# Routing and plan of the shared-and-routed layer inside the stage of its gated products

## What is computed

```
h_shared = swiglu(flat @ shared_in_w.T)          # swiglu(a, b) = silu(a) * b, hidden width 512
out_shared = h_shared @ shared_out_w.T + shared_out_b
g_idx = argmax(flat @ group_gate_w.T + group_bias)          # 2 groups
e_sel = (flat @ expert_gate_w.T)[group g_idx] + expert_bias[g_idx]   # 4 experts of the group
topv, topi = top_k(softmax(e_sel), 2); topv = topv / (sum(topv) + 1e-8)
h_expert = swiglu(flat @ expert_in_w.T)
out = out_shared + sum over the two chosen e: (topv_e * (h_expert @ expert_out_weight[e].T) + expert_out_bias[e])
```

## Time and profile before

| what | value |
|---|---|
| three runs | 3017.52, 3017.73, 3019.3 us |
| median | 3017.73 us |
| the profiled execution's own time | 3008.34 us |
| its span, first to last instruction | 3006.4 us |
| busy in the span: TensorE, VectorE, ScalarE, GpSimd | 80%, 51%, 39%, 17% |
| mean granted TensorE clock | 0.898 |

### The profile page before, as it was taken

The page is one execution under the profiler, slowest core; times in us unless marked ns, Lnnn a source line. Parts: engine busy times, 40 slices in busy tenths (PEclk is TensorE's granted clock), DMA queues, the critical chain, the costliest instruction groups (busy, mean ns, idle before and its releaser), DMA issues. The chain is left out here.

```text
span 3006.4 us, 52688 instructions
## 1 busy us (share of the span) xinstructions
PE 2412.4 (80%) x18555; PEld 2014.1 (67%) x18555; DVE 1548.0 (51%) x3102; ACT 1158.1 (39%) x2239; POOL 501.8 (17%) x812
## 2 busy tenths in 40 slices
PE   6989599769987859874976999999999999963266
PEld 4868499769965734764875777777777777753244
DVE  4646522232236651144445777777777777742455
ACT  3333222112213321122214666666666666624433
POOL 0000022112202100510001122222222222110043
PEclk9999699779988969976997999999999999976577
DMA  5000023134341121321665231335254452022144
GB/s 137 1 1 1 27 85 96 52 97 150 94 101 59 47 92 49 113 67 40 249 257 154 75 109 37 97 93 139 67 143 131 118 147 69 22 60 40 57 138 129
DMA packets 136391, 273.54 MB, mean 91 GB/s; under 512 B 33666, under 2 KB 70568, under 8 KB 133060
## 3 DMA queue, kind: packets, MB, share of 16 engines
q1 hardware_dynamic: 117332, 217.49, 23.2%
q0 software_dynamic: 18800, 52.69, 6.5%
HBM read 466.52 MB, written 65.74 MB: 177 GB/s over the span
## 5 line engine op out<-in xcount | busy, mean ns | idle before, releaser
L2245 PE MATMUL tx_ring<-g_ident,tx_p 128*128 128x128 f32 x2552 | 399.9, 284 | 40.9 <-DVE tx_p_t L2490 8.9
L2245 PEld LDWEIGHTS tx_ring<-g_ident,tx_p 128*128 128x128 f32 x2552 | 287.7, 142 | 147.3 <-DVE tx_p_t L2490 36.6
L2490 DVE COPY tx_p_t<-tx_ring 128x512 f32<-128x512 f32 x464 | 306.6, 686 | 147.3 <-PE tx_ring L2245 144.0
L2483 DVE TENSOR_REDUCE tx_neg_max<-tx_scores 128x1 f32<-128x1354 f32 x232 | 361.2, 1557 | 16.9 <-PE tx_scores L2233 16.7
L2379 ACT ACTIVATE tx_p<-tx_scores,tx_neg_max 128x1354 f32<-128x1354 f32 x232 | 322.6, 1390 | 104.2 <-DVE tx_neg_max L2483 103.9
L2233 PE MATMUL tx_scores<-tx_keys,tx_queries 96*128 96x512 f32 (+1 forms) x696 | 203.2, 401 | 14.5 <-DMA tx_queries<-tx_q_hi 11.2
L2386 ACT ACTIVATE tx_p_t<-tx_ring 128x384 f32<-128x384 f32 x232 | 113.4, 489 | 238.5 <-PE tx_ring L2245 235.3
L2285 PE MATMUL tx_ring<-tx_p_t,tx_values 128*32 128x128 f32 x5104 | 151.9, 274 | 17.4 <-ACT tx_p_t L2386 16.4
L2285 PEld LDWEIGHTS tx_ring<-tx_p_t,tx_values 128*32 128x32 f32 x5104 | 135.9, 110 | 28.3 <-ACT tx_p_t L2386 27.7
L2622 POOL TENSOR_SCALAR tx_std<-tx_mean_var 128x1 f32<-128x1 f32 x58 | 14.8, 256 | 769.5 <-DVE tx_mean_var L2554 403.0
L192 PE MATMUL ln_turned<-g_ident,g_xn 128*128 128x128 f32 x176 | 40.7, 419 | 117.8 <-DVE g_xn L179 117.8
(11 more groups left out here) (961 smaller groups left out, 5197.4 us busy)
## 6 DMA issues: line engine op xcount, KB each, us to landing
tx_keys<-expert_keys SPq DMA_DIRECT2D x696, 169.5 KB
lv1e_w<-in_L_ffn_W SPq DMA_DIRECT2D x232, 256.0 KB
tx_w<-in_L_ffn_W SPq DMA_DIRECT2D x58, 1024.0 KB
lv0e_w<-in_L_ffn_W SPq DMA_DIRECT2D x200, 256.0 KB
tx_values<-expert_values SPq DMA_DIRECT2D x58, 704.0 KB
tx_rows<-in_L_ffn_rows SPq DMA_DIRECT2D x29, 640.0 KB, 3.9
g_adj_t<-in_adj_t POOLq DMA_DIRECT2D x3, 3872.0 KB, 22.1
expert_values<-kv_v SPq DMA_DIRECT2D x8, 1408.0 KB
```

The lines of the kernel that those rows point to most:

```text
L2245: last = nc.tensor.transpose(ring[u % 2][:, (t - t0) * P:(t - t0 + 1) * P], p[n % 2][:, t * P:(t + 1) * P], g.ident[:])
L2483: nc.vector.tensor_reduce(neg_max[:, n % 4:n % 4 + 1], sc[n % 2][:, 0:N], AX_X, ALU.max, negate=True)\
L2490: nc.vector.tensor_copy(p_t[:, n % TURNED, t0:t0 + nt, :], ring[u % 2][:, 0:nt * P].rearrange("p (t q) -> p t q", q=P))\
```

## The change

The stages `srr` and `srp` are gone from `shared_and_routed`. Their instructions stand in a new class `Sorting`, whose methods are called inside `stage_gated_hidden`. TensorE runs the routing products first, then the products of slice 0, the counts, slice 1, four of the turned blocks, slice 2, the inversion of the sort and four more, slice 3 and the last three. VectorE's steps have become a generator that yields behind each step, and `take` draws steps up to a marker: up to "rank" ahead of the gated product of slice 0, up to "found" ahead of that of slice 1, and the rest ahead of that of slice 3. ScalarE's exponential, marks and copies stand between its silu instructions. The comparison `at_spot` is made in two halves. Counts, ranks, found places and logits share one bank of PSUM (`small`), and the turned coefficients use one bank (`turned`) in place of three. The helpers `top_two`, `softmax_to` and `divide_by_sum` became generators, which the other routing stages run to their end at once (`run`), so their instructions stay as they were.

```diff
@@ -1068,6 +1089,7 @@
     full = N // P
     with ExitStack() as ctx:
         s = Pool(nc, ctx, tag)
+        sort = Sorting(nc, g, s, *sorting)
         w, w_loaded = held.w_in, held.w_in_loaded
@@ -1086,14 +1108,17 @@
                 sync.dma_start(g.hidden_dram[b * P:b * P + n, :], h_rows[0:n, b % 3, :]).then_inc(kept[b % 3], 16)
             for k in range(3):
                 sync.wait_ge(kept[k], 16 * ((NB + 2 - k) // 3))
+            sort.rows_kept(sync, None)
 
         @block.gpsimd
         def _(pool):
+            sort.constants(pool)
             nc.gpsimd.memset(h[:, :, NT:NP], 0.0).then_inc(pad, 1)
             pool.wait_ge(pad, 1)
 
         @block.tensor
         def _(pe):
+            sort.pe_logits(pe)
             pe.wait_ge(w_loaded[0], 16)
             for j in range(HT):
@@ -1105,6 +1130,12 @@
                                                     w[0][:, k, half * HID + j * P:half * HID + (j + 1) * P],
                                                     src_t[:, k, c * CW:(c + 1) * CW], start=(k == 0), stop=(k == KD - 1))
                     last.then_inc(done, 1)
+                if j == 0:
+                    sort.pe_rank(pe)
+                if j == 2:
+                    sort.pe_found(pe)
+                if j:
+                    sort.pe_turn(pe, j - 1)
             pe.wait_ge(w_loaded[1], 16)
             for b in range(NB):
@@ -1122,12 +1153,18 @@
 
         @block.scalar
         def _(act):
+            sort.act_exp(act)
             for j in range(HT):
+                if j == 2:
+                    sort.act_marks(act)
+                if j >= 2:
+                    sort.act_turn(act, j - 2)
                 act.wait_ge(a_full, j + 1)
                 if j >= 2:
                     act.wait_ge(h_done, j - 1)
                 nc.scalar.activation(gate[j % 2][:].rearrange("p (c n) -> p c n", c=CH), wide[0][:, :, 0:CW], ACT.Silu)\
                     .then_inc(gate_done, 1)
+            sort.act_turn(act, 2)
             for b in range(NB):
                 act.wait_ge(rows_full, b + 1)
                 if b < 2:
@@ -1138,7 +1175,13 @@
 
         @block.vector
         def _(dve):
+            steps = sort.dve_steps(dve)
+            take(steps, 0, "rank")
             for j in range(HT):
+                if j == 1:
+                    take(steps, 0, "found")
+                if j == 3:
+                    take(steps, 1000)
                 dve.wait_ge(b_full, j + 1)
                 dve.wait_ge(gate_done, j + 1)
                 nc.vector.tensor_tensor(h[:, j, 0:NT].rearrange("p (c n) -> p c n", c=CH), wide[1][:, :, 0:CW],
@@ -1317,10 +1360,9 @@
                     pool.wait_ge(ones, 1)
 
             stage_norm(nc, g, "srn", g.xn, g.xn, g.xn_t, held.affine[:, 0:KD], held.affine[:, KD:2 * KD])
-            stage_route(nc, g, "srr", g.xn_t, experts + 2, "grouped", weights, counts,
-                        held=(held.gates, held.gates_loaded, held.gate_bias, 2))
-            stage_plan(nc, g, "srp", weights, counts[:, :, 0:experts], plan, coef=counts)
-        stage_gated_hidden(nc, g, "srh", g.xn_t, held, h)
+            sorting = (plan, g.xn_t, experts + 2, "grouped", weights, counts[:, :, 0:experts], counts,
+                       (held.gates, held.gates_loaded, held.gate_bias, 2))
+            stage_gated_hidden(nc, g, "srh", g.xn_t, held, h, sorting)
         stage_routed_tiles(nc, g, "sro", h, held, plan, a["L1_ffn_out_bias"])
 
 
@@ -1541,6 +1583,365 @@
+class Sorting:
...
+        self.small, self.turned = s.ps("small", [P, BANK]), s.ps("turned", [plan.width, BANK])
...
+    def pe_rank(self, pe):
+        nc, experts = self.nc, self.plan.experts
+        wide = (NB + 1) * experts
+        pe.wait_ge(self.shaped, 2)
+        pe.wait_ge(self.v_step, 1)
+        flat, counts = self.small[:, 0:wide], self.every[:].rearrange("p b e -> p (b e)")
+        nc.tensor.matmul(flat, self.upto[:], counts[:, NB * experts:], start=True, stop=False)
+        for shift in range(1, NB + 1):
+            before = (NB - shift) * experts
+            last = nc.tensor.matmul(flat, self.all_ones[:], counts[:, before:before + wide], start=False, stop=(shift == NB))
+        last.then_inc(self.rank_full, 1)
+    def pe_turn(self, pe, c):
+        nc = self.nc
+        b0, n = TG[c]
+        pe.wait_ge(self.v_step, 1)
+        if c:
+            pe.wait_ge(self.turned_read, c)
+        for b in range(b0, b0 + n):
+            last = nc.tensor.transpose(self.turned[:, (b - b0) * P:(b - b0 + 1) * P], self.coef[:, b, :], self.g.ident[:])
+        last.then_inc(self.turned_full, 1)
+    def pe_found(self, pe):
+        nc, pairs = self.nc, CHOICES * NB
+        pe.wait_ge(self.marked, 3)
+        pe.wait_ge(self.hot, 3)
+        for n in range(pairs):
+            last = nc.tensor.matmul(self.small[:, 0:3 * self.plan.tiles], self.at_spot[:, n, :],
+                                    self.marks[:, n // NB, n % NB, :, :].rearrange("p r t -> p (r t)"),
+                                    start=(n == 0), stop=(n == pairs - 1))
+        last.then_inc(self.found_full, 1)
+    def act_exp(self, act):
+        values = self.work[3][:, :, 0:4] if self.rule == "grouped" else self.weights[:]
+        act.wait_ge(self.exp_asked, 1)
+        self.nc.scalar.activation(values, values, ACT.Exp).then_inc(self.exp_done, 1)
+    def act_turn(self, act, c):
+        b0, n = TG[c]
+        act.wait_ge(self.turned_full, c + 1)
+        self.nc.scalar.activation(self.plan.coef_t[:, b0 * P:(b0 + n) * P], self.turned[:, 0:n * P], ACT.Copy)\
+            .then_inc(self.turned_read, 1)
+    def act_marks(self, act):
+        marks, in_tile = self.marks, self.in_tile
+        act.wait_ge(self.hot, 1)
+        act.wait_ge(self.v_step, 5)
+        self.nc.scalar.activation(marks[:, :, :, 0, :].rearrange("p c b t -> p (c b) t"),
+                                  in_tile[:].rearrange("p c b t -> p (c b) t"), ACT.Copy, scale=self.one_up[:])\
+            .then_inc(self.marked, 1)
+        self.nc.scalar.activation(marks[:, 1, :, 2, :], in_tile[:, 1, :, :], ACT.Copy).then_inc(self.marked, 1)
...
+    def dve_plan(self, dve):
...
+        dve.wait_ge(shaped, 2)
+        yield "rank"
+        dve.wait_ge(rank_full, 1)
+        link(nc.vector.tensor_copy(count[:], rank[:, NB, :]))
+        yield
...
+        for half in (slice(0, NB), slice(NB, pairs)):
+            nc.vector.tensor_tensor(at_spot[:, half, :],
+                                    spot[:].rearrange("p c b -> p (c b)")[:, half].unsqueeze(2).to_broadcast([P, NB, P]),
+                                    number_f[:].unsqueeze(1).to_broadcast([P, NB, P]), ALU.is_equal).then_inc(hot, 1)
+            yield
...
+        yield "found"
+        dve.wait_ge(found_full, 1)
+        link(nc.vector.tensor_scalar(spare[:], found[:, 0, :], 0.0, None, ALU.is_equal))
+        yield
...
+    def dve_steps(self, dve):
+        yield from self.dve_route(dve)
+        yield from self.dve_plan(dve)
...
+def take(steps, count, marker=None):
+
+    n = 0
+    for at in steps:
+        if at is not None and at == marker:
+            return
+        n += 1
+        if marker is None and n >= count:
+            return
```

More of the change, by code:

```diff
@@ L579, in divide_by_sum, with run @@
     link(nc.vector.tensor_reduce(col, values, AX_X, ALU.add))
+    yield
     if eps is not None:
         link(nc.vector.tensor_scalar(col, col, eps, None, ALU.add))
+        yield
     link(nc.vector.reciprocal(col, col))
+    yield
     link(nc.vector.tensor_tensor(values, values, over(col, width), ALU.mult))
+    yield
+def run(steps):
+    for _ in steps:
+        pass
 def stage_route(nc, g, tag, src_t, width, rule, weights, mask, held, keys=None):
@@ L653, in _ @@
                 link(nc.vector.tensor_tensor(chosen, chosen, other, ALU.add))
-                softmax_to(link, nc, dve, chosen, exps, c0, 4, exp_asked, exp_done, 1)
-                divide_by_sum(link, nc, exps, c0, 4)
+                run(softmax_to(link, nc, dve, chosen, exps, c0, 4, exp_asked, exp_done, 1))
+                run(divide_by_sum(link, nc, exps, c0, 4))
                 picked = work[2][:, :, 4:8]
-                top_two(link, nc, g, exps, picked, work[0][:, :, 0:4], work[1][:, :, 0:4], c0, 4, 2.0)
+                run(top_two(link, nc, g, exps, picked, work[0][:, :, 0:4], work[1][:, :, 0:4], c0, 4, 2.0))
                 link(nc.vector.tensor_tensor(exps, exps, picked, ALU.mult))
-                divide_by_sum(link, nc, exps, c0, 4, 1e-8)
+                run(divide_by_sum(link, nc, exps, c0, 4, 1e-8))
                 for i, group in enumerate((first, second)):
@@ L671, in _ @@
             a, b2 = work[0][:, :, 0:width], work[1][:, :, 0:width]
-            softmax_to(link, nc, dve, logits[:], weights[:], c0, width, exp_asked, exp_done, 1)
+            run(softmax_to(link, nc, dve, logits[:], weights[:], c0, width, exp_asked, exp_done, 1))
             if rule == "logits":
-                top_two(link, nc, g, logits[:], mask[:], a, b2, c0, width, BIG)
```

(11 more changed lines are left out.)

264 lines of the change are left out of this document (added).

## The result

| | before | after |
|---|---|---|
| median of the runs beside each other | 3017.62 us (3015.14 to 3019.3, 4 runs) | 2994.24 us (2987.05 to 2997.82, 4 runs) |
| ratio, 95% interval | | 0.992 (0.9901 to 0.994) |
| the profiled execution's own time | 3008.34 us | 2997.82 us |
| first routing product to first row block | 73.90 us | 50.44 us |
| first routing product to the next stage's first product | 118.87 us | 95.22 us |

The account below looks back on a forecast made before the run. No engine fills the routing-and-plan stretch, a chain from engine to engine before TensorE-bound gated products. Removing 27.67 us, returning 2.95 for matmuls and 0.85 for a stall, gains 23.8: 3017.73 to 2993.9 us, range 2985 to 3001.

Parts of the forecast that it names:

- The sum: 27.67 us stretch goes; 2.95 us of inserted matmuls and a 0.85 us stall come back; net gain 23.87 us.
- the steps: Clock times carried through steps 1 to 6; row blocks start some 50.2 us after the first routing product.
- slow start: First half of slice 0 begins at half clock, taking 6.32 us in place of 4.55, 1.77 more.
- step 1: Slice 0 behind routing products: a half ends at 1091.39, b half at 1095.94; VectorE's routing hidden whole.
- The rival of a start at full clock: Slice 0 follows other TensorE work at once, without slow start; gain 25.3 us, 2992.4 us; chance 0.12.
- steps 2, 3, 5, 6: Matmuls between gated slices at full clock: counts 0.6 us, turned blocks 1.4, inversion 0.95, together 2.95.
- The bound of 5.46 at half clock: Bad end for the inserted matmuls: costing what they did at half clock, 2.5 us more than 2.95.
- step 4: VectorE's place steps delay slice 1's product; TensorE stalls 0.85 us before slice 2's b half.
- the rival of a stretched chain: Each of 35 VectorE place steps takes 0.1 us more; stall grows 3.5, gain 20.3, 2997.4 us; chance 0.07.
- Hidden work: GpSimd's constants done by about 1079.5, table load by 1088.5, VectorE's nine last steps by 1119.7; none cost time.
- Everything after shifts whole: Downstream stages keep their lengths and start earlier, since nothing is tied to a clock and weights are in place.
- The forecast of 2984.5 us for the profiled execution: The 3008.34 us of the profiled execution before, carried to the changed kernel; from the median the forecast is 2993.9 us.

Follow-up runs that it names:

- late shares: Changed kernel with VectorE's 13 place steps behind the spots taken only ahead of the product of slice 2; stretch 49.07 us, own time 2987.57 us.
- six and ten more steps: Changed kernel with six or ten repeats of one VectorE multiplication ahead of the marker found; stretches 53.78 and 54.94 us, own times 2996.38 and 2993.25 us.
- in a row: Changed kernel, but TensorE does routing, counts, turns and inversion and awaits VectorE's last step before slice 0; 3009.76 us against 3015.68 before (0.9982).
- a dense half first: Late shares kernel with slice 0's a half ahead of the routing products, counts behind slice 1's a half; stretch 47.05 us, own time 2986.20 us.
- the third one: Third profile of the changed kernel, no edit, run beside the last experiment; own time 2985.36 us, stretch 50.44 us, median 2985.69 us (0.9908).
- woven kernel: Dense half first kernel with VectorE's products of slices 0 and 1 earlier, counts and inversion later; 2985.30 us against 3014.61 (0.9909), again 2985.87 (0.9909).

## Why the prediction was right

- *The sum.* Local gain forecast 23.87 us; measured 23.46 in the stretch and 23.65 up to the next stage. The mechanism came out as forecast, and the terms were each off by a few tenths that partly cancel: the inserted matmuls 0.33 us cheaper, the stall 0.52 dearer, the rest of the routing products and slices 0.22 longer. The medians gave 23.4, 26.2 and 27.1, so that the first lies within 0.4 us of the forecast is luck. The prediction also has two figures for its stretch: the sum gives 73.90 - 23.87 = 50.03 us, the steps 50.2. The steps put the slow first half at 6.32 us up to ScalarE's start, which holds the hand-over to ScalarE. By TensorE's own starts all four slices took 37.97 us before, 1.57 more than 4 x 9.10, and not 1.77.
- *Slice 0 and the slow start (step 1).* Routing products and slice 0 were put at 19.13 us together. They took 19.08 (1076.53 to 1095.61), and 19.04 again. Their parts came out otherwise: 7.22 and 11.86 where I had 8.26 and 10.87. With the change the half clock is one period of 10.2 us that starts 1.3 to 2.6 us into the routing products and ends in slice 0; in the kernels with the late shares and with six and ten more steps, which have this part alike, the sum is 19.04 to 19.08 too. Taking the slow start of the old gated products as a fixed 1.77 us came close by luck: it is no separate cost, and in the kernel "in a row" the same products needed 5.6 us in place of 2.9 to reach full clock, which cost 1.3 us more. The rival of a start at full clock is refuted: 0.50 from 1080 to 1087, with slice 0 starting at 1083.75, behind products that had kept TensorE busy all the time. The advice of the Trainium skill, page "TensorE: Matmul & The Clock Gate", section "Why this matters for your kernels", to keep TensorE busy without a gap, is not enough here: the trace shows the clock falling during unbroken work of 10-column products (1.00 at 1077, 0.50 from 1080), and in the kernel with a dense half first holding to their end (1086.56).
- *Inserted matmuls (steps 2, 3, 5, 6).* Counts 0.51, turned blocks 0.43, 0.43 and 0.33, inversion 0.92, each from its start to the next piece's: 2.62 us in place of 2.95. The bound of 5.46 at half clock did not come.
- *The stall (step 4).* 0.85 forecast; 1.10 us of idle time measured, and 1.37 us in the stretch, as the late shares show. The size was off, mostly by a hand-over that I had put at hundredths: VectorE's product of slice 0 starts at 1095.98, 0.37 us after TensorE has gone on to its next piece at 1095.61. What these 0.37 us consist of, the trace doesn't show. VectorE's own terms were right: 12.42 us of place steps, where the forecast had 12.4. They take 12.42 us in the kernel "in a row" too, where TensorE is idle for two thirds of them, so the rival of a stretched chain falls. The six and ten more steps show that this rival had named the right weak point, and priced it too low: a longer chain would also have cost the clock.
- *Hidden work.* The constants ended at 1079.06, the table load at 1087.39 and the last plan step at 1119.83, each before it was wanted. No wait names them.
- *Downstream.* "Everything after shifts whole" agrees with the timed runs: the 23.65 us lie in all three intervals (18 to 30, 22 to 36 and 23 to 32 us). In the one pair of profiled executions it seemed to fail by 13.7 us, which is about the scatter of one kernel there (13.6). The forecast of 2984.5 us for the profiled execution missed the first profile (2997.82) for that reason, and that the third one came near it (2985.36) is luck as well.

## What to carry to other kernels

Where a stage that one engine bounds stands next to one that another engine bounds, and neither needs the other's results, lay them over each other piece by piece; the borders and GpSimd's constants were worth 2.9 us here, the overlap over 20. Then write each hand-over as a race between the two engines' sums from a common point, and cut the longer chain at the last result that somebody waits for. Judge a change of under 1% in one stage by that stage's own stretch, which repeated to 0.04 us here, and not by the difference of two profiled executions: those of the changed kernel alone scattered by over 12. A stretch in which the clock changes can scatter too: that of the woven kernel did by 1.7 us.

## What the runs showed of the hardware

- The granted clock of TensorE can fall in the midst of unbroken work: from 1.00 to 0.50, 1.3 to 2.6 us into 44 narrow products (10 columns), for 10.2 us in all, in the six profiles that have this order. With a dense half of 4.6 us ahead, it fell only within the last 0.7 us of the narrow products or at their end, for 3.4 us in two profiles and 6.8 in a third.
- A stall may cost its length and, on top, some time at half clock. After 1.10 us idle the clock stayed at 1.00; after 2.79 and 3.94 us it had read 1.00 while TensorE was idle and dropped to 0.50 as work began again or 1 us later, for 3.4 us both times, which cost 1.7 us.
- VectorE's steps of 0.15 to 0.25 us took the same beside a TensorE that was busy all the time as beside one that was idle for two thirds of it: 12.42 us for the same 35 place steps both times.
